# Fused Mamba, attention and mixture-of-experts layer: three row normalisations on ScalarE cut into four pieces each and set between exponentials

## What is computed

```python
xn = _layernorm(x, axis=-1)
...
x = x + mla(rmsnorm(x, w_ln1), ...)      # latent attention, 16 heads, causal
x = x + moe(rmsnorm(x, w_ln2), ...)      # shared expert, and 7 routed experts, the top 2 of each row
...
def rmsnorm(x, w):
    norm = jnp.sqrt(jnp.mean(x * x, axis=-1, keepdims=True)) + EPS
    return x / norm * w
```

## Time and profile before

| what | value |
|---|---|
| median of 3 runs | 4334.64 us (4331.84 to 4338.19) |
| the profiled execution, its own time | 4341.7 us |
| its span | 4339.9 us |
| mean granted TensorE clock over the span | 0.939 |
| PE busy | 3742.1 us (86%), 22264 matmuls |
| DVE busy | 2956.6 us (68%) |
| ACT busy | 2513.7 us (58%) |
| POOL busy | 2196.6 us (51%) |

### The profile page before, as it was taken

The page is one execution under the profiler, slowest core; times in us unless marked ns, Lnnn a source line. Parts: engine busy times, 40 slices in busy tenths (PEclk is TensorE's granted clock), DMA queues, the critical chain, the costliest instruction groups (busy, mean ns, idle before and its releaser), DMA issues. The chain is left out here.

```text
span 4339.9 us, 70850 instructions
## 1 busy us (share of the span) xinstructions
PE 3742.1 (86%) x22264; PEld 2767.9 (64%) x22264; DVE 2956.6 (68%) x5456; ACT 2513.7 (58%) x6505; POOL 2196.6 (51%) x1115
## 2 busy tenths in 40 slices
PE   5888888888888874899969999998999998999986
PEld 2344444444444442777758888887888887888876
DVE  3454454555444522222259999999999999999998
ACT  1443343434343441233358888888888888888874
POOL 3223333333333322000038788778778778878774
PEclk8899998999898987999989999999999999999998
DMA  3322222222232312666622212212222222222221
GB/s 91 98 80 84 80 92 86 88 80 81 79 101 81 93 46 75 199 208 208 211 92 98 88 68 100 93 66 97 93 70 93 93 81 82 93 88 75 93 83 38
DMA packets 286365, 417.03 MB, mean 96 GB/s; under 512 B 78261, under 2 KB 250678, under 8 KB 263672
## 3 DMA queue, kind: packets, MB, share of 16 engines
q1 hardware_dynamic: 273048, 381.12, 27.2%
q0 software_dynamic: 12288, 33.57, 2.2%
q10 hardware_dynamic: 864, 0.10, 0.0%
HBM read 330.63 MB, written 83.17 MB: 95 GB/s over the span
## 5 line engine op out<-in xcount | busy, mean ns | idle before, releaser
L1536 POOL TENSOR_TENSOR m_ub<-m_Bb,m_dtx 128x2048 f32<-128x2048 f32 x254 | 1156.9, 4566 | 280.3 <-PE m_Y L1904 176.4
L1645 ACT ACTIVATE m_dA<-m_dt,m_a_neg 128x128 f32<-128x128 f32 x4096 | 1211.1, 388 | 129.4 <-DVE m_S L1756 129.0
L1904 PE MATMUL m_Y<-m_ub,m_ident 128*128 128x128 f32 x8192 | 955.8, 278 | 62.4 <-DVE m_ub L1733 62.0
L1904 PEld LDWEIGHTS m_Y<-m_ub,m_ident 128*128 128x128 f32 x8192 | 939.3, 194 | 73.1 <-DVE m_ub L1733 72.8
L543 ACT ACTIVATE f_pt<-f_X 128x512 f32<-128x512 f32 (+1 forms) x704 | 371.8, 555 | 730.3 <-PE f_X L845 699.1
L618 DVE TENSOR_REDUCE f_nm<-f_Y 128x1 f32<-128x512 f32 (+3 forms) x896 | 434.0, 531 | 378.3 <-PE f_Y L845 354.1
L1748 DVE SCALAR_TENSOR_TENSOR m_PR<-m_dA,m_S 128x512 f32<-128x512 f32 x512 | 355.9, 695 | 25.7 <-POOL m_ub L1536 7.4
L1748 DVE SCALAR_TENSOR_TENSOR m_S<-m_dA,m_PR 128x512 f32<-128x512 f32 x512 | 354.8, 693 | 12.0
L1756 DVE CUSTOM_DVE_ANT_1 m_S<-m_S,m_ub 128x512 f32<-128x512 f32 x512 | 353.3, 690 | 0.6 <-issue 0.6
L1756 DVE CUSTOM_DVE_ANT_1 m_PR<-m_PR,m_ub 128x512 f32<-128x512 f32 x512 | 353.3, 690 | 0.2 <-DVE m_PR L1748 0.2
L828 PE MATMUL f_Y<-f_kst,f_qst 96*128 96x512 bf16 (+3 forms) x1024 | 256.2, 331 | 109.0 <-DVE f_nm L618 90.4
(11 more groups left out here) (234 smaller groups left out, 6369.2 us busy)
## 6 DMA issues: line engine op xcount, KB each, us to landing
m_Bb<-m_bc_dram SPq DMA_DIRECT2D x64, 1024.0 KB, 4.6
m_Cb<-m_bc_dram SPq DMA_DIRECT2D x64, 1024.0 KB, 6.4
f_parts_dram<-f_parts SPq DMA_DIRECT2D x32, 768.0 KB, 4.1
f_kst<-f_parts_dram SPq DMA_DIRECT2D x192, 128.0 KB, 2.6
f_qst<-f_parts_dram SPq DMA_DIRECT2D x192, 128.0 KB, 2.6
e_rows<-sorted_rows SPq DMA_DIRECT2D x70, 256.0 KB, 2.8
e_wg<-Wg SPq DMA_DIRECT2D x70, 256.0 KB, 2.9
e_wu<-Wu SPq DMA_DIRECT2D x70, 256.0 KB, 4.0
```

The source lines that it names most:

```text
L1536: pool.tensor_tensor(ub[:, h, i, :, :], Bb[:, s, :, :], dtx[:, m, None, s * SN:(s + 1) * SN].to_broadcast([P, NST, SN]), ALU.mult).then_in ...
L1645: last = act.activation(dA[:, h, i, n, :], dtt[:, par, m, s * SN:(s + 1) * SN], ACT.Exp, scale=a_neg[:, m, n:n + 1])
L1904: last = pe.matmul(Y[:, i * SN:(i + 1) * SN], ident[:, :], ub[:, h, 1 + i, n, :], start=False, stop=(n == NST - 1), skip_group_check=True)
```

## The change

`h1a`, `h2a` and `xn` become four entries of the table each, with the piece as their index `i`; each issues one instruction instead of four. The waits stand ahead of piece 0, and the semaphore is raised by piece 3. The pieces' numbers are: h1a 12, 13, 14, 15 (it was 13), h2a 29, 30, 31, 32 (it was 30), xn 38, 40, 41, 44 (it was 36). `T` moves from 15 to 16. All other entries stay. The lines behind the change move by three (L566 becomes L568, L778 becomes L781, L834 becomes L837).

```diff
-                          (11, "h1", 0, 0), (12, "scat", 0, 0), (12, "rl1", 1, 0), (13, "h1a", 0, 0), (15, "T", 0, 0),
+                          (11, "h1", 0, 0), (12, "scat", 0, 0), (12, "rl1", 1, 0), (12, "h1a", 0, 0), (13, "h1a", 1, 0), (14, "h1a", 2, 0), (15, "h1a", 3, 0), (16, "T", 0, 0),
...
             if kind == "h1a":
                 sc1 = sc1_[:, parity(kind, r), :, :]
-                act.wait_ge(x_loaded, 16 * (b + 1))
-                act.wait_ge(sc_step, 10 * b + 10)
-                for t in range(TT):
-                    last = act.activation(h1[:, t, :], xm[:, t, :], ACT.Identity, scale=sc1[:, 7, t:t + 1], bias=sc1[:, 10, t:t + 1])
-                last.then_inc(h1_done, 1)
+                if i == 0:
+                    act.wait_ge(x_loaded, 16 * (b + 1))
+                    act.wait_ge(sc_step, 10 * b + 10)
+                part = act.activation(h1[:, i, :], xm[:, i, :], ACT.Identity, scale=sc1[:, 7, i:i + 1], bias=sc1[:, 10, i:i + 1])
+                if i == TT - 1:
+                    part.then_inc(h1_done, 1)
...
             if kind == "h2a":
-                act.wait_ge(rms2_rec, b + 1)
-                act.wait_ge(scattered, 16 * TT * TOPK * b)
-                for t in range(TT):
-                    last = act.activation(h2[:, t, :], x2[:, t, :], ACT.Copy, scale=sc2[:, 4, t:t + 1])
-                last.then_inc(h2_done, 1)
+                if i == 0:
+                    act.wait_ge(rms2_rec, b + 1)
+                    act.wait_ge(scattered, 16 * TT * TOPK * b)
+                part = act.activation(h2[:, i, :], x2[:, i, :], ACT.Copy, scale=sc2[:, 4, i:i + 1])
+                if i == TT - 1:
+                    part.then_inc(h2_done, 1)
```

More of the change, by code:

```diff
@@ L152, in build_attn @@
     for n, kind, i, j in ((0, "xload", 0, 0), (0, "mvx", 0, 0), (0, "sl1", 1, 0), (1, "stack1", 1, 0), (4, "mvs", 0, 0), (6, "rp1", 1, 0), (7, "ro1", 1, 0), (8, "bn", 0, 0),
-                          (11, "h1", 0, 0), (12, "scat", 0, 0), (12, "rl1", 1, 0), (13, "h1a", 0, 0), (15, "T", 0, 0),
[1 row of a table added]
                           (18, "lat", 0, 0), (18, "ym1", 1, 0), (19, "scat", 1, 0), (21, "kq", 0, 0), (24, "kq", 0, 1), (25, "wo", 0, 0),
-                          (26, "split", 0, 0), (28, "mid", 0, 0), (29, "h2", 0, 0), (30, "h2a", 0, 0), (31, "xrload", 0, 0),
-                          (32, "keep", 0, 0), (33, "ht", 0, 0), (35, "route", 0, 0), (36, "lg", 0, 0), (36, "xn", 0, 0), (37, "g", 0, 0), (37, "stack", 0, 0),
-                          (39, "u", 0, 0), (40, "rank", 0, 0), (42, "g", 1, 0), (43, "u", 1, 0), (45, "kq", 1, 0),
[3 rows of a table added]
                           (47, "kq", 1, 1), (47, "pfx", 0, 0), (49, "split", 1, 0), (50, "nm", 0, 0), (51, "d", 0, 0), (53, "mid", 1, 0), (53, "nmt", 0, 0),
@@ L549, in do @@
                 sc1 = sc1_[:, parity(kind, r), :, :]
-                act.wait_ge(x_loaded, 16 * (b + 1))
-                act.wait_ge(sc_step, 10 * b + 10)
-                for t in range(TT):
-                    last = act.activation(h1[:, t, :], xm[:, t, :], ACT.Identity, scale=sc1[:, 7, t:t + 1], bias=sc1[:, 10, t:t + 1])
-                last.then_inc(h1_done, 1)
-            if kind == "xn":
-                act.wait_ge(xn_done, 2 * b + 1)
-                act.wait_ge(xr_loaded, 16 * (b + 1))
-                act.wait_ge(xs_ready, b)
-                for t in range(TT):
-                    last = act.activation(xn[:, t, :], xr[:, t, :], ACT.Identity, scale=mvx[:, t, 0:1], bias=mvx[:, t, 1:2])
-                last.then_inc(xn_done, 1)
-            if kind == "h2a":
-                act.wait_ge(rms2_rec, b + 1)
-                act.wait_ge(scattered, 16 * TT * TOPK * b)
-                for t in range(TT):
-                    last = act.activation(h2[:, t, :], x2[:, t, :], ACT.Copy, scale=sc2[:, 4, t:t + 1])
-                last.then_inc(h2_done, 1)
+                if i == 0:
[4 more added lines that the diff above has]
+                    part.then_inc(h1_done, 1)
+            if kind == "xn":
+                if i == 0:
+                    act.wait_ge(xn_done, 2 * b + 1)
+                    act.wait_ge(xr_loaded, 16 * (b + 1))
+                    act.wait_ge(xs_ready, b)
+                part = act.activation(xn[:, i, :], xr[:, i, :], ACT.Identity, scale=mvx[:, i, 0:1], bias=mvx[:, i, 1:2])
+                if i == TT - 1:
+                    part.then_inc(xn_done, 1)
+            if kind == "h2a":
+                if i == 0:
+                    act.wait_ge(rms2_rec, b + 1)
+                    act.wait_ge(scattered, 16 * TT * TOPK * b)
+                part = act.activation(h2[:, i, :], x2[:, i, :], ACT.Copy, scale=sc2[:, 4, i:i + 1])
+                if i == TT - 1:
+                    part.then_inc(h2_done, 1)
             if kind == "T":
```

## The result

The changed kernel is slower: 4377.78 us median of 5 runs (4375.70 to 4397.23) against 4338.19 us (4331.84 to 4352.11) for the kernel before, run beside it. The ratio is 1.0096, with a 95% interval from 1.0076 to 1.0117. I had said 4350.4 us, at most 4371. The profiled execution was the longest of the five, 4397.23 us with a span of 4395.4; its mean granted clock was 0.930, that of the other four 0.934 to 0.936.

What follows compares the result with a forecast made beforehand. PE was taken as the engine a round waits for, with ACT idle over half the time. Terms 14.4 + 1.4 + 0 = +15.8 us on a median of 4334.6 gave 4350.4 us, 0.36% slower; range 4334 to 4371.

Steps and rivals of the forecast that it cites:

- h2, place B: PE's wait before transposing h2: two exponentials delay the last piece 0.96 us in 15 rounds, +14.4 us.
- rival on the half clock: Behind h2's transposing: three more rounds fall to 1.2 GHz, 6.2 us each, giving 4369 us; chance 0.18.
- h1, place A: Transposing of h1: 0.96 us later, 0.98 us of PE work moved ahead; `lat` 0.1 us later in 14 rounds, +1.4 us.
- xn: Behind h2's transposing: Tanh and DVE's L750 come 1 us earlier, but L754 waits for the second projection; 0 us.
- Switching functions: On ACT, pieces using Identity and Copy alternate with Exp without any gap, so this costs 0 us.
- DVE ahead: Rival: earlier Tanh removes PE's waits of 0.24 and 0.82 us in 15 rounds, 4334.5 us or faster; chance 0.13.
- absorbed: Rival: a later PE wait swallows the 0.96 us at h2, or the edit does nothing; 4336 us; chance 0.11.

Runs made afterwards that it cites:

- only_xn: Kernel before with only the pieces of xn spread (38, 40, 41, 44), h1 and h2 whole: 4332.57 us, ratio 0.9985.
- h2_whole_late: Kernel before with the four activations of h2 kept together but two steps later, at 32 instead of 30: 4393.36 us, ratio 1.0119.
- after_filled: Changed kernel with six matmuls of ones ahead of PE's wait for h2: 4311.84 us, ratio 0.9938 to the kernel before.
- after_ones_behind: Changed kernel with six matmuls of ones behind the transposing of h2, ahead of the routing: 4353.03 us, ratio 1.0020 to the kernel before.
- best: Changed kernel with h2 whole at 28 and `mid` of the first pair moved to 31; h1 and xn stay spread: 4294.18 us, ratio 0.9895 to the kernel before.
- h1_and_xn: Changed kernel with h2 whole again at 30; h1 and xn stay spread: 4312.66 us, ratio 0.9937 to the kernel before.
- h2_first: Kernel before with the four activations of h2 whole at 28, ahead of `mid`: 4318.11 us, ratio 0.9957.
- ht_34: Changed kernel with the transposing of h2 at 34 instead of 33, one s1 item ahead of it: 4348.68 us, ratio 1.0021 to the kernel before.
- only_h2: Kernel before with only the pieces of h2 spread (29, 30, 31, 32), h1 and xn whole: 4402.65 us, ratio 1.0150.

## Why the prediction was wrong

Its sign was right and its size was not: a loss of 0.36% was said, 0.96% measured, outside the range.

- **h2, place B (+14.4 us): the mechanism right, its term incomplete.** Piece 0 where the four had been, two exponentials ahead of the last piece, PE with nothing else to do: the wait grew from 0.86 to 1.83 us, and from 9.7 to 20.4 us over the twelve rounds, 10.7 where 12 x 0.96 = 11.5 was meant. That is all that the sum had for the place.
- **The step that failed** is the sentence of the rival on the half clock: "the same waits came before both kinds of round, so 0.96 us need not tip it", and the count of three more rounds that went with it. It tipped it in nearly every round. The stretches without any half clock behind place B went from seven of twelve to none, and they have 71.3 us more at 1.2 GHz in the twelve rounds. That is worth up to half its length, 36 us, and PE's busy time grew by 30.5 us, where three rounds at 6.2 us had been thought of as the bad case and the sum had nothing. The half clock should have been a term of the sum. The trace of before had the evidence: behind this place, with its two waits close together, the clock fell in five rounds of twelve, three times by a long stretch. The prediction also took the first wait as 1.43 us throughout; it was 2.9 us in two rounds of before and in five of the changed kernel, and in three of these five the clock fell there, ahead of the wait for h2.
- **h1, place A (+1.4 us): wrong in sign.** The order was as predicted, 3.17 us behind piece 0, with the s1 item and s2(4,1) in the gap, and the wait stayed at 1.1 us. A small loss at `lat` is there, larger than forecast: 6.7 us in four rounds instead of 0.1 in each. But it spared half clock (21.4 to 3.4 us behind the place), and by itself h1 spread is 0.24% faster (0.08 to 0.41).
- **xn (0): right.** 0.9985, with an interval that holds 1. In a good round of only_xn the Tanh comes 6.7 us behind the transposing of h2, where it was 7.8, and L757 still 10.1 behind it, where L754 was 10.3; PE's waits behind it stayed, at 0.33 and 0.82 us in the changed kernel. In the changed kernel itself the forecast of DVE's wait (2.5 us a round) was wrong, 3.7, for a reason that isn't xn's.
- **Switching functions (0): right.** The rows alternate with no gap, and h2_whole_late loses as much without alternating.
- **The rivals.** "DVE ahead" and "absorbed" fell. "More of the half clock" was the right one, with 0.18 for a chance and too small a price.

The sum made again with what was measured, for the profiled execution: 4341.7 + 50.1 in the twelve rounds is 4391.8, and 4397.2 was seen; the 5.4 us between lie behind this stage, which ended 50.0 us later than before. For the 39.6 us between the medians the traces give no such sum.

The Trainium skill's sentence ("TensorE: Matmul & The Clock Gate", "Part 1: The HAM clock gate"), that "the default state is throttled, and activity releases the throttle", agrees with after_filled and after_ones_behind as far as they go: added matmuls bring the half clock from 450.6 us to 279.9 and 327.7. The same section puts the penalty of the ramp, the warming up of a cold engine, under 1% of a typical span. Here it isn't paid once but in the rounds: the stage has 368.6 us at half clock before the change, worth up to 184 us, 4.2% of the span, in rounds in which PE is busy 85% of the time.

## What to carry to other kernels

Where PE is the engine that a round waits for, look at the granted clock behind each of its waits, and count the rounds in which it falls there: a place where it falls in a few is one where another microsecond of waiting may cost several. Price a delay there as its own length plus the stretch at half clock in every round (here 0.9 us of waiting and 2.5 us of slower matmuls a round), and look first for work of PE that can be moved into the wait. If there is none, a few matmuls without a use, ahead of the wait, may be worth more than they cost. It has to be measured each time: they bought 1.6% in the changed kernel, 0.7% in the kernel before, 0.6% in best, and in h1_and_xn nothing that the intervals can tell. Count the half clock in more than one place, too: where h2's wait was taken away (h2_first), some of it moved to place A.

## What was not expected of the hardware

One more microsecond of waiting ahead of the transposing, in rounds in which PE is busy 85% of the time, took the rounds with half clock behind it from five of twelve to all twelve. Once it has begun, the half clock can outlast the cause by far: in the row at 1147.40 above PE has no idle time in 16 us, and the clock is at 1.2 GHz for 12.9 of them. Four matmuls of ones in a round (1.04 us) took best from 0.9895 to 0.9839, in a place where PE didn't wait, and to 0.9840 from behind the transposing. How the clock weighs what PE did just before is not settled by these runs, nor why ht_34, with the wait of before, has more of the half clock behind the place than before had; its new wait at the routing may have a part in it, which no run shows. What was shown is that a later h2 is enough to bring the half clock on (only_h2, h2_whole_late), that added matmuls take most of it away with h2 just as late (after_filled), and that they shorten it from within (after_ones_behind).
